# Attention B: elu + 1 from one unscaled copy, by ScalarE and GpSimd instead of VectorE

## What is computed

```python
def _sigma(x):
    return jax.nn.elu(x) + 1.0
...
def step(carry, qkv):
    M, z = carry
    q, k, v = qkv
    sq = _sigma(q)
    denom_q = jnp.sum(sq * z[:, :, None, :], axis=-1, keepdims=True) + EPS
    A_mem = jnp.matmul(sq, M) / denom_q
    scores = jnp.matmul(q, jnp.swapaxes(k, -2, -1)) * inv_sqrt_dk
    scores = jnp.where(causal, -jnp.inf, scores)
    A_dot = jnp.matmul(jax.nn.softmax(scores, axis=-1), v)
    A_s = beta * A_mem + (1.0 - beta) * A_dot
    sk = _sigma(k)
    denom_k = jnp.sum(sk * z[:, :, None, :], axis=-1, keepdims=True) + EPS
    V_prev = jnp.matmul(sk, M) / denom_k
    M_new = M + jnp.einsum('bhtk,bhtv->bhkv', sk, v - V_prev)
    z_new = z + jnp.sum(sk, axis=-2)
    return ((M_new, z_new), A_s)
```

## Time and profile before

| | before |
|---|---|
| median of three runs | 1655.88 us |
| the three runs | 1643.7, 1655.88, 1659.46 us |
| span of the profiled execution | 1651.6 us |
| PE busy | 1435.0 us (87%) |
| DVE busy | 1192.2 us (72%) |
| ACT busy | 872.1 us (53%) |
| POOL busy | 924.7 us (56%) |
| attention B's part of the span | about 960 to 1651.6 us |

### The profile page before, as it was taken

One profiled execution on the slowest core, in us unless ns is written; L12 is line 12 of the kernel. 1 busy time (PEld: TensorE's weight loads), 2 busy tenths in 40 slices (PEclk: granted clock), 3 DMA queues, 4 the chain that ended last, 5 costly groups with the idle time before them and its releaser, 6 DMA issues. The chain is left out here.

```text
span 1651.6 us, 46495 instructions
## 1 busy us (share of the span) xinstructions
PE 1435.0 (87%) x13604; PEld 1237.1 (75%) x13668; DVE 1192.2 (72%) x3330; ACT 872.1 (53%) x2019; POOL 924.7 (56%) x1340
## 2 busy tenths in 40 slices
PE   6999999999999999996677737888888888888886
PEld 4899989999989999886465525766766676666665
DVE  4468788788878888875245437888888888888775
ACT  2466667666666766654466623444444444444441
POOL 4466667767767776654588734444444444444431
PEclk9899999999999999998799959999999999999998
DMA  4523333222333322220444223333333333333330
GB/s 134 161 78 100 88 95 95 85 83 82 93 86 95 95 86 82 78 77 14 124 135 124 77 76 97 103 105 109 103 102 104 107 105 105 104 106 107 108 101 17
DMA packets 181693, 158.10 MB, mean 96 GB/s; under 512 B 12529, under 2 KB 163185, under 8 KB 181618
## 3 DMA queue, kind: packets, MB, share of 16 engines
q1 hardware_dynamic: 181618, 157.17, 33.2%
HBM read 113.09 MB, written 44.04 MB: 95 GB/s over the span
## 5 line engine op out<-in xcount | busy, mean ns | idle before, releaser
L609 PE MATMUL a_bank<-a_vp,a_prob 128*128 128x74 f32 x4096 | 600.6, 253 | 0.0
L609 PEld LDWEIGHTS a_bank<-a_vp,a_prob 128*128 128x128 f32 x4096 | 590.6, 193 | 5.6
L697 DVE TENSOR_REDUCE a_nmax<-a_bank 128x2 f32<-128x512 f32 x512 | 345.1, 685 | 155.3 <-PE a_bank L578 155.1
L496 ACT ACTIVATE a_prob<-a_bank 128x512 f32<-128x512 f32 x512 | 305.4, 596 | 209.0 <-PE a_bank L593 203.8
L578 PE MATMUL a_bank<-a_k_st,a_q_st 96*128 96x256 bf16 x1024 | 261.5, 279 | 32.8 <-DVE a_nmax L697 25.6
L593 PE MATMUL a_bank<-a_q_st,a_k_st 120*128 120x256 bf16 x1024 | 282.2, 276 | 2.0 <-POOL a_q_st L345 2.0
L1638 PE MATMUL c_o_bank<-c_vb,c_prob 128*128 128x96 f32 x1024 | 169.9, 289 | 17.9 <-DVE c_ad L1921 14.0
L1797 DVE TENSOR_REDUCE c_nmax<-c_bank 128x4 f32<-128x512 f32 x256 | 164.8, 685 | 18.1 <-PE c_bank L1608 15.6
L1503 ACT ACTIVATE c_prob<-c_bank 128x256 f32<-128x256 f32 x256 | 98.8, 386 | 141.8 <-PE c_bank L1588 140.4
L416 POOL TENSOR_TENSOR a_prod<-a_ov,a_wgt 128x512 f32<-128x512 f32 x128 | 152.2, 1189 | 34.1 <-POOL a_prod L416 17.2
L345 POOL TENSOR_SCALAR a_q_st<-a_mt 24x2048 bf16<-24x2048 bf16 x64 | 121.4, 1896 | 87.4 <-ACT a_mt L470 51.6
(11 more groups left out here) (207 smaller groups left out, 2862.2 us busy)
## 6 DMA issues: line engine op xcount, KB each, us to landing
a_q_st<-scratch_a_parts_dram SPq DMA_DIRECT2D x64, 288.0 KB
a_k_st<-scratch_a_parts_dram SPq DMA_DIRECT2D x192, 96.0 KB
c_q_st<-scratch_c_parts_dram SPq DMA_DIRECT2D x64, 288.0 KB
c_k_st<-scratch_c_parts_dram SPq DMA_DIRECT2D x192, 96.0 KB
scratch_a_parts_dram<-a_parts SPq DMA_DIRECT2D x32, 384.0 KB, 2.7
scratch_c_parts_dram<-c_parts SPq DMA_DIRECT2D x32, 384.0 KB, 2.7
a_x<-in_x SPq DMA_DIRECT2D x32, 128.0 KB, 3.1
scratch_y<-a_y SPq DMA_DIRECT2D x32, 128.0 KB, 2.7
```

The costliest lines, as they stand in the source:

```text
L496: act.activation(prob[h % 4][:, :, :].rearrange("p a b -> p (a b)"), t_ps[h % 2][:, :], ACT.Exp).then_inc(exped, 1)
L609: mm = pe.matmul(o_ps[g % 2][:, at:at + VM], prob[h % 4][:, c, t * P:(t + 1) * P], vp[o][:, c, 0:VM], start=c == 0, stop=c == NT - 1)
L697: dve.tensor_reduce(nmax[:, t, 2 * g:2 * g + 2, 0], s_ps[t][:, :].rearrange("p (h k) -> p h k", h=2), AX.X, ALU.max, negate=True).then_inc ...
```

## The change

Before, four instructions on PSUM and one on SBUF made the inputs of sg. After it, ACT copies k and q out of PSUM in one instruction with no scale; POOL makes pos = max(kq, 0) from that copy; ACT exponentiates kq itself; POOL takes the minimum with 1 (tile one), and adds. DVE's two instructions are gone. The factor HD ** -0.5 moves into the exponential of the scores (L1503). PE waits no longer for pos and neg before it writes ps_a. The new copy waits for the sg of two batches before, and POOL waits for its own sg before xb.

```diff
-        USES_A = [(at_d, 2, 3), (kq_d, 2, 0), (mt_d, 2, 1)]
+        USES_A = [(at_d, 2, 3), (kq_d, 1, 0), (mt_d, 2, 1)]
...
                 if active(j, u, 0):
 
+                    apart(pool, spare)
+                    pool.tensor_scalar(pos[:, :, :], kq[i][:, :, :], 0.0, 0.0, ALU.max, ALU.add).then_inc(sg_n, 1)
                     pool.wait_ge(nexp_d, n + 1)
+                    apart(pool, spare)
+                    pool.tensor_scalar(one[:, :, :], nexp[:, :, :], 1.0, 0.0, ALU.min, ALU.add).then_inc(sg_n, 1)
+                    pool.wait_ge(sg_n, 2 * (n + 1))
                     if later(j, n, 2):
                         pool.wait_ge(read_p, (n - 1) * 3)
                     pool.tensor_tensor(sg[i][:, :, :, :].rearrange("p s a t -> p a s t"),
                                        pos[:, :, :].rearrange("p a (s t) -> p a s t", s=NS),
-                                       nexp[:, :, :].rearrange("p a (s t) -> p a s t", s=NS), ALU.add
+                                       one[:, :, :].rearrange("p a (s t) -> p a s t", s=NS), ALU.add
                                        ).then_inc(sg_d, 1)
+                    pool.wait_ge(sg_d, n + 1)
...
-                        act.activation(prob[g % 4][:, :], t_ps, ACT.Exp).then_inc(exped, 1)
+                        act.activation(prob[g % 4][:, :], t_ps, ACT.Exp, scale=HD ** -0.5).then_inc(exped, 1)
...
-                        act.copy(kq[i][:, 0, :], ps_a[:, 0:T]).then_inc(kq_d, 1)
-                        act.mul(kq[i][:, 1, :], ps_a[:, T:2 * T], HD ** -0.5).then_inc(kq_d, 1)
+                        if later(j, n, 2):
+                            act.wait_ge(sg_d, n - 1)
+                        act.copy(kq[i][:, :, :].rearrange("p a t -> p (a t)"), ps_a[:, :]).then_inc(kq_d, 1)
...
-                        act.wait_ge(pn_d, (n + 1) * 2)
+                        act.wait_ge(kq_d, n + 1)
...
-                        act.activation(nexp[:, :, :], neg[:, :, :], ACT.Exp).then_inc(nexp_d, 1)
+                        act.activation(nexp[:, :, :], kq[i][:, :, :], ACT.Exp).then_inc(nexp_d, 1)
...
                         free(pe, USES_A, 1, j, u)
-                        if later(j, n, 1):
-                            pe.wait_ge(pn_d, n * 2)
...
                                 free(pe, USES_A, 2, j, u)
-                                pe.wait_ge(pn_d, 2 * min(n + 1, NB) if isinstance(j, int) else 2 * (n + 1))
...
-                    if s == 1 and active(j, u, 0):
-                        dve.wait_ge(kq_d, (n + 1) * 2)
-                        if later(j, n, 1):
-                            dve.wait_ge(sg_d, n)
-                        dve.tensor_scalar(flat(pos), ps_a[:, :], 0.0, None, ALU.max).then_inc(pn_d, 1)
-                        dve.tensor_scalar(flat(neg), ps_a[:, :], 0.0, None, ALU.min).then_inc(pn_d, 1)
```

More of the change, by code:

```diff
@@ L1204, in attention_b @@
         q_st, k_st = two("q_st", [P, H, T], BF16), two("k_st", [P, H, T], BF16)
-        pos, neg, nexp = (sb(a, [P, 2, T]) for a in ("pos", "neg", "nexp"))
+        pos, one, nexp = (sb(a, [P, 2, T]) for a in ("pos", "one", "nexp"))
         sg = two("sg", [P, NS, 2, SEG])
@@ L1238, in attention_b @@
         kq_p, kq_d = sem("kq_p"), sem("kq_d")
-        pn_d, nexp_d, sg_d = sem("pn_d"), sem("nexp_d"), sem("sg_d")
+        sg_n, nexp_d, sg_d = sem("sg_n"), sem("nexp_d"), sem("sg_d")
         split_d, parts_out = sem("split_d"), sem("parts_out")
@@ L1428, in body @@
                 if active(j, u, 0):
-                    pool.wait_ge(kq_d, (n + 1) * 2)
+                    pool.wait_ge(kq_d, n + 1)
                     if later(j, n, 2):
```

## The result

The changed kernel is slower: 1676.8 us (median of five runs, 1669.0 to 1714.9) against 1655.9 (by now five runs, 1643.7 to 1659.5), ratio 1.0107 with a 95% interval of 1.007 to 1.0144. A second set gave 1.0114 (1.0062 to 1.0165). The forecast was 1641 us with a range to 1658.

The account below looks back on a forecast made before the run. PE and DVE waiting for each other bound attention B, with w4's start deciding. 29 units x 0.5 us = 14.5 us; 1655.9 - 14.5 = 1641.4, say 1641 us, range 1630 to 1658.

Parts of the forecast that it names:

- What bounds the kernel: In attention B, PE and DVE waiting for each other bound the 20.13 us unit; neither is full.
- the start of w4 as the deciding quantity: DVE's reduction w4 starts at 1317.63 in the timeline; what the change moves it earlier, the unit gains.
- DVE's lead of 1.0 us: Without pos and neg on DVE, reduction w2 starts at about 1310.9, not 1311.90, and DVE's following work moves with it.
- the held cast: DVE's cast L1784 is held by POOL's last split L1443, ends at 1314.98; work behind comes 0.63 us earlier, not 1.0.
- The price of pos and one: Each new POOL instruction taken at 0.62 us, from L1440, a tensor_scalar of the same 512 elements.
- My upper bound: Highest price for pos and one on POOL: 1.26 us, from L1455, a two-input operation.
- POOL's later work: sg, xb, next norm and shift come later; ACT's L1554 about 0.4 us late, hidden by 0.82 us idle.
- the price without cover: Without ACT's idle time before the exponential, the lateness of L1554 would cost 0.4 us a unit.
- Rival C: POOL's pos and one cost as much as L1455, delaying L1766: 3 to 32 us slower, about 1671; chance 0.08.
- The forecast at its own price: With pos and one near 0.62 us, w4 starts at about 1317.1, gaining 0.5 us a unit; chance 0.50.
- Rival A: POOL's one gets between DVE's two L1766: gain 0.2 us a unit, 6 us, time 1650; chance 0.20.
- The copy and scale: ACT saves about 0.1 us, all in idle time; the scale in L1503 adds at most 0.02, eight times a unit.

## Why the prediction was wrong, point by point

- *What bounds the kernel, and the start of w4 as the deciding quantity*: right. The kernels in which shift comes in time and nothing meets DVE later follow it: w4 at 7.66 gives units of 20.1, 7.03 gives 19.5, 6.63 gives 19.2, 8.30 gives 20.7.
- *DVE's lead of 1.0 us and the held cast*: right. w2 starts at 0.91, the cast takes 0.53 and ends at 5.00 (forecast 4.98).
- *The price of pos and one* is the step that failed. I took 0.62 us from L1440 "as the form is the same but for the output type". It was not the same: L1440 multiplies and adds, and the two new ones do not. They take 1.93 each, which puts shift 3.0 us later and the unit at +0.6 us instead of -0.5. My upper bound, 1.26 from a two-input operation, was too low as well; a bound taken from the nearest rows is none where the operation itself has no row.
- *POOL's later work, "costed at nothing"*: failed by the same error. 0.82 us of idle time on ACT was the cover, the lateness 2.4 us. I had named the price without cover and made no rival of it, though it was the chain to ask about for any price above mine.
- *Rival C* had the right sign and cause (dearer instructions) and the wrong place. I let it act through L1766; the slow form held the two up by 0.22 us only, and the loss came through shift and z. That its 1671 lies near the measured 1676.8 is luck.
- *The forecast at its own price*, 0.5 us a unit: wrong too. It got nothing (unit 20.1). Rival A was the true course, with 0 instead of 0.2, as rs was 0.26 us later than I worked out.
- *A meeting I did not look for*: L1817 with sg, 0.38 us. I checked the instructions around w4 and not where sg itself would move to.
- *The copy and scale*: about as said; the run with them alone gained 0.08 us a unit, which the sum had put at nothing.
- *The clock* was not in the sum at all. Units in which it fell were 1.4 to 3.1 us longer than those of the same kind at full clock, in the two profiles of the changed kernel.

## What to carry to other kernels

Price an operation only from a row with the same operation codes; the same engine, shape and instruction name are not enough, and where there is no such row the upper bound has to be far above the neighbours. When work leaves VectorE, list what it then meets on GpSimd: a neighbour missed by 0.16 us is a meeting as soon as anything moves, and the order of GpSimd's long and short instructions decided 1.2 us a unit here. For each engine that gets work, follow its last instruction to the one that waits for it and compare the lateness with that wait's slack.

## What the runs showed of the hardware that I had not expected

- GpSimd's tensor_scalar of 512 fp32 elements: 0.62 us for multiply and add, 1.50 for a single maximum or multiply, 1.93 to 1.95 for the three other pairs timed. Why the one pair is fast stays open.
- The slow form holds VectorE up for little of its time: pos ran from 1112.72 to 1114.65 and the two L1770 inside it took 0.82 us, whereas cheap pos and one of 0.62 each made them 1.26. With pos, one and sg last, L1817 and a cast ran inside `one` in their usual 0.31 and 0.17. The Trainium skill (SBUF — State Buffer, "Who interferes with whom") has the first comer hold the shared pair of ports for its whole instruction; for the fast form and for tensor_tensor the traces agree, for this one not.
- A two-input VectorE instruction with both inputs in SBUF waits for GpSimd's sg as well, at both sizes seen: 16 elements took 0.86 us instead of 0.17, 144 elements 0.69 instead of 0.31.
- PE's clock stayed at 1.00 from the fourth unit of attention B to the last copy in the kernels with units of 19.2 to 20.7 us, and fell again and again in the two kernels in which PE waits for z's lateness in front of L1590 (1.3 to 1.6 us a unit). Not every unit with that wait was followed by a fall; what decides it stays open.
